# A ViT-like tower on one core: router logits out of the matmuls that turn h, the last expert stage with units on partitions, the quantised MLP's steps split anew, semaphores cleared late

## The reference

```python
h = h + _L0_attn_ref(_layernorm(h), ...)     # linear attention
h = h + _L0_ffn_ref(_layernorm(h), ...)      # "grouped": 16 experts, 4 a token, and a shared one
h = h + _L1_attn_ref(_layernorm(h), ...)     # mamba in both directions
h = h + _L1_ffn_ref(_layernorm(h), ...)      # quantised MLP
h = h + _L2_attn_ref(_layernorm(h), ...)     # group attention
h = h + _L2_ffn_ref(_layernorm(h), ...)      # "shared": 8 experts, 2 a token, and a shared one
h = h + _L3_attn_ref(_layernorm(h), ...)     # collaborative attention
h = h + _L3_ffn_ref(_layernorm(h), ...)      # "geluexp": 8 experts, 2 a token

def _L3_ffn_ref(x, router_w, w1, w2):
    probs = softmax(x @ router_w.T)
    weights, sel = top_k(probs, 2)
    y[e] = gelu(x[tokens of e] @ w1[e]) @ w2[e]       # 192 -> 768 -> 192
    out = zeros.at[token].add(weights * y[sel])

def _L1_ffn_ref(x0, ...):                     # round(clip(., -8, 7)) is the quantisation
    xq = round(clip(x0 / mean(alpha_a1), -8, 7))
    x1 = gelu((xq @ wq1.T) * alpha_w1 * mean(alpha_a1) + b1)
    hq = round(clip(clip(x1, -10, 10) / mean(alpha_a2), -8, 7))
    return (hq @ wq2.T) * alpha_w2 * mean(alpha_a2) + b2
```

## Time and profile before

| what | value |
|---|---|
| median of 3 runs | 2660.38 us (2652.83 to 2673.17) |
| the profiled execution | 2658.45 us |
| its span | 2656.7 us |
| mean granted TensorE clock | 0.855 of full speed |
| busy share of the span: PE, DVE, ACT, POOL | 82%, 56%, 39%, 45% |
| routes, from the first to the last instruction | 221 to 296, 1690 to 1746, 2300 to 2353 |
| `quantised_mlp`, main block | 1445 to 1523 |
| `geluexp`'s expert stage, blocks | 2404 to 2625 |

### The profile page before, as it was taken

One profiled execution on the slowest core, in us unless ns is written; L12 is line 12 of the kernel. 1 busy time (PEld: TensorE's weight loads), 2 busy tenths in 40 slices (PEclk: granted clock), 3 DMA queues, 4 the chain that ended last, 5 costly groups with the idle time before them and its releaser, 6 DMA issues. The chain is left out here.

```text
span 2656.7 us, 31829 instructions
## 1 busy us (share of the span) xinstructions
PE 2177.1 (82%) x10180; PEld 1526.2 (57%) x10180; DVE 1476.8 (56%) x2384; ACT 1047.0 (39%) x2332; POOL 1183.1 (45%) x915
## 2 busy tenths in 40 slices
PE   7897529957899999999876599779987999828996
PEld 5565217735555565655435388645664677616774
DVE  6464404444999999999975655331244255421223
ACT  3213103316888888888832433211211033311120
POOL 1200365532898989898963710040233055141111
PEclk9696659957999999999995689589896899758997
DMA  7003123340111111111100000310121000331112
GB/s 266 11 1 79 38 77 101 99 139 33 49 49 49 36 46 49 49 49 49 49 17 25 11 2 1 83 49 0 55 81 34 1 1 1 74 112 43 34 35 78
DMA packets 73268, 136.45 MB, mean 51 GB/s; under 512 B 12809, under 2 KB 60056, under 8 KB 68181
## 3 DMA queue, kind: packets, MB, share of 16 engines
q1 hardware_dynamic: 59030, 108.90, 13.6%
q0 software_dynamic: 14080, 25.53, 2.9%
HBM read 91.14 MB, written 46.28 MB: 52 GB/s over the span
## 5 line engine op out<-in xcount | busy, mean ns | idle before, releaser
L1756 POOL TENSOR_TENSOR mamba_seen<-mamba_state,mamba_c_all 128x774 f32<-128x774 f32 x256 | 440.6, 1739 | 85.3 <-DVE mamba_state L2053 81.3
L2053 DVE TENSOR_TENSOR_SCAN mamba_state<-mamba_decay,mamba_inject_ps 128x774 f32<-128x774 f32 x256 | 450.0, 1758 | 1.9 <-ACT mamba_decay L1962 1.9
L1836 PE MATMUL mamba_y_ps<-mamba_seen,bimamba_ident 128*128 128x387 f32 x1024 | 376.2, 489 | 1.7 <-POOL mamba_seen L1756 1.5
L1962 ACT ACTIVATE mamba_decay<-mamba_dt,mamba_A 128x256 f32<-128x256 f32 x768 | 329.6, 499 | 10.6 <-DVE mamba_state L2053 9.0
L2039 DVE TENSOR_TENSOR mamba_inject_ps<-mamba_dtu,mamba_b_ps 128x774 f32<-128x774 f32 x256 | 248.1, 969 | 22.9 <-PE mamba_b_ps L1822 13.7
L1836 PEld LDWEIGHTS mamba_y_ps<-mamba_seen,bimamba_ident 128*128 128x128 f32 x1024 | 176.6, 192 | 86.8 <-POOL mamba_seen L1756 4.3
L2744 POOL TENSOR_TENSOR collab_keys<-collab_k_all,collab_mixing 108x1548 f32<-108x1548 f32 (+1 forms) x32 | 89.8, 2827 | 137.5 <-issue 79.7
L1372 DVE COPY geluexp_mlp_turned<-geluexp_mlp_turned_ps 128x768 f32<-128x768 f32 x40 | 38.3, 958 | 176.0 <-PE geluexp_mlp_turned_ps L1296 176.0
L1254 POOL DMA_INDIRECT geluexp_z<-geluexp_mlp_sent_rows,geluexp_mlp_rows x40 | 38.9, 973 | 190.2 <-DVE geluexp_mlp_sent_rows L1380 185.0
L1822 PE MATMUL mamba_b_ps<-mamba_parts,bimamba_sel 128*128 128x258 bf16 x256 | 71.9, 281 | 61.9 <-DVE mamba_inject_ps L2039 58.4
L1287 PE MATMUL geluexp_mlp_hid_ps<-geluexp_up,geluexp_mlp_xt 96*128 x320 | 112.7, 495 | 0.1
(11 more groups left out here) (683 smaller groups left out, 4879.7 us busy)
## 6 DMA issues: line engine op xcount, KB each, us to landing
mamba_c_all<-mamba_c SPq DMA_DIRECT2D x32, 1032.0 KB, 5.5
grouped_xs<-embed_empty SPq DMA_DIRECT2D x1, 7760.0 KB, 27.6
grouped_mlp_rows<-grouped_xs SPq DMA_DIRECT2D x20, 388.0 KB
grouped_x_tok<-grouped_z SPq DMA_DIRECT2D x16, 384.0 KB, 6.5
geluexp_up<-in_geluexp_up SPq DMA_DIRECT2D x1, 4608.0 KB
geluexp_down<-in_geluexp_down SPq DMA_DIRECT2D x1, 4608.0 KB
shared_xs<-embed_empty SPq DMA_DIRECT2D x1, 3880.0 KB, 34.1
geluexp_xs<-embed_empty SPq DMA_DIRECT2D x1, 3880.0 KB, 40.5
```

The costliest lines, as they stand in the source:

```text
L1756: pool.tensor_tensor(seen[:, s % SEEN_BUFS].rearrange("p (c n) -> p c n", c=IC), state[:, s % STATE_BUFS].rearrange("p (c n) -> p c n", c=IC),
L1836: mm = pe.matmul(y_ps[:, i, 0:PART], ident[:], seen[:, s % SEEN_BUFS, i * PART:(i + 1) * PART], start=False, stop=(n == STATES - 1))
L1962: ins = act.activation(decay[:, buf, c, :, a:b], by_item(dt[:, t % 2])[:, c, :, a:b], ACT.Exp, scale=A[:, back(t), c, n:n + 1])
L2053: dve.tensor_tensor_scan(flat[0], flat[1], flat[2], 0.0, ALU.mult, ALU.add).then_inc(sem["scanned"], 1)
```

## The change

Four parts. (1) In the route h is turned by a plain fp32 matmul whose moving operand is the identity with the router weights beside it (`turn`), so that the sums h x W of both halves come out next to the turned chunk; pairs of chunks (`TPAIRS`, 9) and four PSUM banks take the place of groups and two. VectorE adds the two partial sums per pair, and at the end makes (L - mean x column sums of W) x rstd + bias of them in four linked ops instead of two. `logits` goes. xn is only written where it is used (grouped, shared; not `geluexp`), and off the way to the logits. (2) `geluexp` gets its own `ungated_blocks`: VectorE copies the block's up weights into `held`, `climb` takes these as stationary and the rows as moving operand, so that units come out on partitions and gelu's result goes into `descend` as it is. (3) In `quantised_mlp` ACT scales the input, GpSimd's three ops become two, VectorE's four become three. (4) The clears come behind the block's GpSimd instructions.

```diff
@@ Stage.block
         with self.nc.Block(no_gpsimd_drain=True) as block:
+            yield block
             if zeroed:
                 @block.gpsimd
                 def _(pool):
                     for s in zeroed:
                         pool.sem_clear(s)
-            yield block
@@ route, SP
+                sp.dma_start(turn[:, 0, W:W + HALF], dram["ident"][0:HALF, 0:HALF]).then_inc(turn_loaded, 16)
+                sp.dma_start(turn[:, 0, 0:W], dram[name + "_router_w"][:, 0]).then_inc(turn_loaded, 16)
+                sp.dma_start(turn[:, 1, 0:HALF], dram["ident"][0:HALF, 0:HALF]).then_inc(turn_loaded, 16)
+                sp.dma_start(turn[:, 1, HALF:HALF + W], dram[name + "_router_w"][:, 1]).then_inc(turn_loaded, 16)
                 sp.dma_start(ident[:], dram["ident"]).then_inc(loaded, 16)
-                sp.dma_start(w[:], dram[name + "_router_w"]).then_inc(loaded, 16)
@@ route, TensorE
+                def turn_h(j):
...
+                    if j >= 4:
+                        pe.wait_ge(normed, j - 3)
+                    for i in range(cn):
                         for m in range(2):
-                            mm = pe.transpose(ht(g, i, n)[:, m * HALF:(m + 1) * HALF], h[:, m, chunk_cols(c0 + i)],
-                                              ident[0:HALF, 0:HALF])
+                            at = i * PLACE + m * (W + HALF)
+                            mm = pe.matmul(ht_ps[0:n, j % 4, at:at + W + HALF], h[:, m, chunk_cols(c0 + i)], turn[:, m, :],
+                                           start=True, stop=True)
...
-                for g in range(len(TGROUPS)):
-                    turn_x(g)
-                    if g + 2 < len(TGROUPS):
-                        turn_h(g + 2)
-                    logits(g)
+                pe.wait_ge(turn_loaded, 64)
+                for j in range(4):
+                    turn_h(j)
                 pe.wait_ge(consts, 5)
+                for m in range(2):
+                    mm = pe.matmul(w_sums, ones32[:], w[m], start=(m == 0), stop=(m == 1))
+                mm.then_inc(sums_done, 1)
+                for j in range(4, len(TPAIRS)):
+                    turn_h(j)
+                pe.wait_ge(loaded, 48)
+                if xn_used:
+                    for ch in range(EARLY + 9):
+                        turn_x(ch)
...
                 pe.wait_ge(taken_ready, 1)
@@ route, ACT
+                for j in range(LAST_PAIR + 1):
+                    roots(j)
+                    if j >= 2:
+                        repeat(j - 2)
+                if xn_used:
+                    for ch in range(EARLY):
+                        evacuate(ch)
                 act.wait_ge(exp_in_ready, 1)
                 act.activation(f["exps"][:], f["logits"][:], ACT.Exp).then_inc(exp_ready, 1)
+                repeat(LAST_PAIR - 1)
+                repeat(LAST_PAIR)
+                if xn_used:
+                    for ch in range(EARLY, TC):
+                        evacuate(ch)
@@ route, VectorE, normalise
+                    dve.tensor_copy(L[0:n, c0:c0 + cn, :], partial(j, 0, n)).then_inc(half_ready, 1)
+                    dve.wait_ge(std_ready, j + 1)
                     dve.reciprocal(rstd[0:n, c0:c0 + cn], std[0:n, c0:c0 + cn]).then_inc(rstd_ready, 1)
+                    dve.wait_ge(half_ready, j + 1)
+                    dve.tensor_tensor(L[0:n, c0:c0 + cn, :], L[0:n, c0:c0 + cn, :], partial(j, 1, n), ALU.add)
...
+                link(dve.tensor_tensor(f["scores"][:], last(mv[:, :, 0], W), over(w_sums, W), ALU.mult))
+                link(dve.tensor_tensor(L[:], L[:], f["scores"][:], ALU.subtract))
+                link(dve.tensor_tensor(L[:], L[:], last(rstd[:], W), ALU.mult))
+                link(dve.tensor_tensor(L[:], L[:], over(b["logit_bias"][:], W), ALU.add))
@@ ungated_blocks (U = 6, PER = 3, HIDS = 3), TensorE
+                def climb(b):
+                    pe.wait_ge(held_ready, b + 1)
+                    pe.wait_ge(xt_ready, b + 1)
+                    if b >= 2:
+                        pe.wait_ge(hid_ready, b - 1)
+                    for u in range(U):
+                        for j in range(2):
+                            mm = pe.matmul(hid_ps[:, b % 2, u // PER, (u % PER) * BLK:(u % PER + 1) * BLK],
+                                           held[:, b % 2, j, u * 128:(u + 1) * 128], xt[:, b % 2, j, :],
+                                           start=(j == 0), stop=(j == 1))
+                    mm.then_inc(up_done, 1)
...
+                for b in range(NB + 1):
+                    if b < NB:
+                        climb(b)
+                    if b + 2 < NB:
+                        turn_x(b + 2)
+                    if b:
+                        descend(b - 1, pe.value_load(home[0:1, b - 1:b], min_val=0, max_val=E - 1))
@@ ungated_blocks, VectorE
+                def hold(b):
+                    e = dve.value_load(home[0:1, b:b + 1], min_val=0, max_val=E - 1)
+                    if b >= 2:
+                        dve.wait_ge(up_done, b - 1)
+                    dve.tensor_copy(held[:, b % 2], up[:, :, ds(e * HID, HID)]).then_inc(held_ready, 1)
...
+                for b in range(NB):
+                    if b + 2 < NB:
+                        hold(b + 2)
+                    dve.wait_ge(y_done, b + 1)
...
@@ quantised_mlp, GpSimd
+                    pool.wait_ge(sem["scaled"], t + 1)
+                    pool.tensor_scalar(xs[:, t % 2], xs[:, t % 2], HIGH, LOW, ALU.min, ALU.max).then_inc(
+                        sem["xs_step"], 1)
+                    pool.wait_ge(sem["xs_step"], t + 1)
...
+                    pool.tensor_scalar(xq[:, t % 2], xs[:, t % 2], ROUND, ROUND, ALU.add, ALU.subtract).then_inc(
                         sem["xq_ready"], 1)
@@ quantised_mlp, ACT
+                def scale_input(t):
+                    if t >= 2:
+                        act.wait_ge(sem["xq_ready"], t - 1)
+                    act.activation(xs[:, t % 2], xn[:, :, cols(t)], ACT.Copy, scale=inv_a[0:HALF, 0:1]).then_inc(
+                        sem["scaled"], 1)
...
                 for t in range(TILES):
                     if t + 1 < TILES:
                         gelu(t + 1)
+                    if t + 2 < TILES:
+                        scale_input(t + 2)
                     copy_out(t)
@@ quantised_mlp, VectorE: three ops for four (min and scale; min/max; add/subtract)
```

More of the change, by code:

```diff
@@ L701 @@
 TGROUPS = tuple((c, min(4, TC - c)) for c in range(0, TC, 4))
+TPAIRS = tuple((c, min(2, TC - c)) for c in range(0, TC, 2))
 ROW = D + 2
@@ L839, in logits @@
[L839 to L846, removed]
-                    mm.then_inc(logits_done, 1)
-                pe.wait_ge(loaded, 64)
@@ L863, in _, with roots @@
                           stop=True).then_inc(place_done, 1)
+                if xn_used:
+                    for ch in range(EARLY + 9, TC):
+                        turn_x(ch)
             @block.scalar
             def _(act):
-                def roots(g):
-                    c0, cn = TGROUPS[g]
+                def roots(j):
+                    c0, cn = TPAIRS[j]
                     n = chunk_rows(c0)
@@ new lines, in repeat @@
+                def repeat(j):
+                    c0, cn = TPAIRS[j]
+                    n = chunk_rows(c0)
+                    act.wait_ge(normed, j + 1)
+                    for i in range(1, k):
+                        act.activation(x_tok[0:n, c0:c0 + cn, i, 0:D], x_tok[0:n, c0:c0 + cn, 0, 0:D], ACT.Copy)
+                LAST_PAIR = len(TPAIRS) - 1
+                act.wait_ge(consts, 4)
+                for j in range(LAST_PAIR + 1):
+                    roots(j)
+                    if j >= 2:
+                        repeat(j - 2)
@@ L955, in _ @@
-                dve.wait_ge(loaded, 64)
-                dve.wait_ge(consts, 11)
-                dve.wait_ge(logits_done, len(TGROUPS))
-                L = f["logits"]
-                n = E
-                dve.tensor_tensor(L[0:TAIL, TC - 1, :], logits_ps[0:TAIL, TC - 1, :], b["logit_bias"][0:TAIL],
-                                  ALU.add).then_inc(chain, 1)
-                count[0] += 1
-                link(dve.tensor_tensor(L[:, 0:TC - 1], logits_ps[:, 0:TC - 1, :],
-                                       b["logit_bias"][:].unsqueeze(1).broadcast_to([BLK, TC - 1, W]), ALU.add))
+                for j_ in range(len(TPAIRS)):
+                    if j_ + 1 < len(TPAIRS):
+                        measure(j_ + 1)
+                    normalise(j_)
@@ L1463, in grouped_experts @@
         weights = (r["weights"], 16 * len(prefetch))
-        route(nc, dram, h, xn, "grouped", E, K, 0, choose, prefetch, r["weights"], r["x_tok"], r["pos"], r["pick"], r["home"])
+        route(nc, dram, h, xn, "grouped", E, K, 0, choose, prefetch, r["weights"], r["x_tok"], r["pos"], r["pick"], r["home"], True)
         xs, z = dram["grouped_xs"], dram["grouped_z"]
@@ L1507, in shared_experts @@
         weights = (r["weights"], 16 * len(prefetch))
```

(2 more changed lines are left out.)

290 lines of the change are left out of this document (211 added, 79 removed).

## The result

Median of four runs 2570.14 us (2564.54 to 2577.47), before 2661.86 in the same comparison: ratio 0.9652, 95% interval 0.9613 to 0.9691. The profiled execution took 2571.77 us with a span of 2570.0, so 86.7 us less span than before. Five more runs beside nine of before gave 0.9659 (0.9637 to 0.9681). The forecast was 2581 in a range of 2563 to 2606.

What follows compares the result with a forecast made beforehand. Limits differ by stage: TensorE in geluexp's expert stage, VectorE and TensorE waiting for each other in the routes. -41.2 - 24 - 3 - 11 = -79 on 2658.45 gives 2579, 2581 on the median's footing; range 2563 to 2606.

Steps and rivals of the forecast that it cites:

- Rival C: Last expert stage of geluexp: the new climb's weight loads are not hidden, 0.22 us a record, +80 for -24, 2685 us; chance 0.03.
- The rule of the Trainium skill that stood against this part: geluexp's climb: a weight load overlaps matmuls in flight only when going to another row group; all 24 go to the same.
- Rival D: geluexp's expert stage: shorter matmuls bring the granted clock to 0.50, 9.7 us a block, +172, 2777 us; chance 0.02.
- The loads are the same four small DMAs before the first matmul: Routes: the small loads ahead of TensorE's first matmul stay the same, on the same queue.
- The pair: Routes: VectorE sets the time of a pair of chunks, 1.9 us, within bounds of 1.6 and 2.6.
- The charge of 1.4 us for ACT's table load: Routes using xn: evacuations and table load before Exp partly stick out, 0.5 us in shared and 0.9 in grouped.
- Rival B: Routes: they stay bound by hand-over, VectorE's own waits cost 2.6 us a pair or more, half the gain goes, 2601; chance 0.13.
- The ring through gelu and ACT's order: quantised_mlp: scale_input(t+2) stands behind gelu(t+1), which needs xq of t+1; the ring takes 9.2 to 11.5 us, taken as 10.5.
- the loop does not get shorter: quantised_mlp: with a ring of 10.5 us against a tile every 10.3 or so, only start and tail gain, -3 us.
- min/max and add/sub on GpSimd 2.5 to 3.4 and 1.9 to 3.3: quantised_mlp: assumed times in us of GpSimd's two remaining ops a tile, longer while VectorE works.
- Rival A: quantised_mlp: GpSimd's loop gets shorter by a whole op, -19 us in place of -3, 2565 us; chance 0.07.
- At a block's end GpSimd has long been idle: Clears: moved to the block's end they cost nothing, as GpSimd is idle or its sequencer runs ahead of its DMAs.

## Why the prediction was right, and where its terms were off

**Part 2** stands term by term: 0.112 a record, 4.86 a block forecast and 4.85 measured, -24 and a microsecond of clears forecast, -26.2 measured; 24.2 by the run with the stage undone. Rival C is refuted: with 24 weight loads into the same row group a record costs 0.112, not 0.22. The rule of the Trainium skill that stood against this part ("TensorE: Matmul & The Clock Gate", Part 3, "The mechanism") doesn't hold for these loads. (The same section also lets a load into a background weight buffer go ahead of matmuls in flight, which the rows would fit; no run here shows which it is.) Rival D fell too, at a clock of 1.00.

**Part 1** came out at -46.1 for -41.2, by two errors that go against each other. The sentence "The loads are the same four small DMAs before the first matmul" failed: they are four, but the two biases that are broadcast no longer stand among them, and TensorE starts 1.3, 3.2 and 2.5 us earlier, 7.0 that no term had; the run with all loads waited for gave 9.6 back. In return `top` comes 21.4, 20.7 and 20.6 us after TensorE's start instead of 20.0, 19.4 and 19.4. The pair was sized well (1.79 for 1.9); the waits for TensorE were not: the first statistics come 2.1 us after its start, and VectorE idles 0.79 us before the second pair of each route and 0.41 before the fifth in grouped and geluexp. ACT's root holds VectorE up in shared's route alone, by 0.3. That Part 1 came out near its forecast is thus partly luck: without the earlier start it is about -39. The charge of 1.4 us for ACT's table load did not fall due: it still lies beside VectorE's links, and from `top` to the end the routes take no longer than before (36.3, 16.4 and 13.7 us for 36.4, 16.8 and 13.8). Rival B is refuted by the rows of the route, and the run with two banks shows the price of it.

**Part 3**: mechanism right, size off. The ring through gelu and ACT's order is there, and cutting it gave 11.3 us. The sentence that "the loop does not get shorter" failed, by a term that was mis-sized, "min/max and add/sub on GpSimd 2.5 to 3.4 and 1.9 to 3.3". Min/max takes 0.76 where VectorE idles or does its reciprocal, and 1.09 on average. I took its price from L2217 and L2220, which have the same columns but a multiply or an add in the pair. Add/subtract takes 3.37 within the ring, just above its upper end. Hence 9.3 to 9.8 a tile instead of 10.5, and -6.1 to -6.9 instead of -3. ACT's scaling took 0.87 for the 0.8 forecast, but that was luck: by its columns the row that it was estimated from (3.40 for six gelus of 344) gives 1.13 for 688. Rival A (-19) did not come about, for the reason given against it.

**Part 4**: in the norms -8.9 for -7.4; the difference is the clock in mamba's out norm, which the sum had left out. In the quantised block and geluexp's expert stage the run with the clears first gives 1.9 and 2.2 for 1.8 together: in the first 1.2 of it comes with the clock in the last tile, in the second the same code differs by 1.5 from execution to execution. In linear attention and grouped's dense block nothing came, where 1.8 were forecast. "At a block's end GpSimd has long been idle" failed for the dense block. Linear attention's first matmul does come 0.8 us earlier (0.39 us into the stretch for 1.16), but the granted clock also falls to 0.50 earlier there, at 107.8 us into the stretch for 109.8; that this is what takes the 0.8 back was not tried.

The rest is not the change's. Collab's projections took 98.7 us in the changed kernel and 93.0 before, at clocks of 0.81 and 0.87; but in the runs above, with the same code there, they took 93.0, 95.9 or 98.7 from execution to execution, and collab attention 168 to 172. This spread is about that of the runs' times.

## What to carry to other kernels

Where two engines hand work back and forth, look first at how far the faster one can run ahead: here the number of banks stayed at four, but halving it in the new order cost 41.6 of the 46.1 us won. Price an operation from a row of the same kind on the same engine, not of the same shape. Before moving a step onto an engine, write down its order and look for a ring: a scaling of 0.87 us behind gelu instead of ahead of it cost 11 us.

## What the runs showed of the hardware that was not expected

- GpSimd's tensor_scalar on 96 x 688 fp32: 0.76 us for min and max, 2.5 for add and subtract, where VectorE idles or does its reciprocal; beside VectorE's other ops mostly 1.1 to 1.7 and 3.1 to 4.2. With multiply and min in place of min and max it takes 3.08 on average for 1.09.
- Plain fp32 matmuls in place of transposes did not raise the granted clock of the route: 0.50 before and after, with TensorE busy for 15.64 of 21 us.
- In mamba's out norm the granted clock fell to 0.50 at 1.6, 4.2 or 7.3 to 7.9 us into the stretch, and from its first matmul the stage took 23.6, 23.3 or 21.6 to 22.2 us. The 4.2 are the two kernels that clear first, the 1.6 the one with `quantised_mlp` as before; what sets the moment is open.
